# A two-layer graph network on one core: input rows turned by 32x32 blocks on the vector engine instead of by matmul, and head 0's value parts packed

## The reference

```
feats = einsum('bnf,hfu->bhnu', x, W0)
e_self, e_neigh = feats . a_self, feats . a_neigh              # per head and node
dense  = leaky_relu(e_self[i] + e_neigh[j], 0.2) + (-1e10) * (1 - adj[i, j])
x = layernorm(x + relu(softmax_j(dense) @ feats + bias))        # layer 0
agg = (adj @ x) / max(rowsum(adj), 1e-6)
x = layernorm(x + relu(concat([x, agg]) @ W1.T))                # layer 1
```

## Time and profile before

| | us |
|---|---|
| median of 3 runs | 3260.62 |
| profiled execution, its own time | 3259.45 |
| span of its profile | 3257.7 |
| PE busy | 3198.1 (98%) |
| PEld busy | 2698.7 (83%) |
| DVE busy | 2351.7 (72%) |
| ACT busy | 2095.9 (64%) |
| POOL busy | 283.6 (9%) |

### The profile page before, as it was taken

The page is one execution under the profiler, slowest core; times in us unless marked ns, Lnnn a source line. Parts: engine busy times, 40 slices in busy tenths (PEclk is TensorE's granted clock), DMA queues, the critical chain, the costliest instruction groups (busy, mean ns, idle before and its releaser), DMA issues.

```text
span 3257.7 us, 124901 instructions
## 1 busy us (share of the span) xinstructions
PE 3198.1 (98%) x56896; PEld 2698.7 (83%) x56896; DVE 2351.7 (72%) x4272; ACT 2095.9 (64%) x2712; POOL 283.6 (9%) x251
## 2 busy tenths in 40 slices
PE   7999999999999999999999999999999999999998
PEld 6969789697896978979788797987969879697895
DVE  6858678586785857859588585876858768586685
ACT  5748567485674947749477494765837658485583
POOL 0010200102011020100202002020020200202001
PEclk8999999999999999999999999999999999999999
DMA  6143151431524225251242513415144251331512
GB/s 217 58 114 102 51 159 66 109 98 51 154 68 118 87 60 157 62 133 65 78 141 63 140 56 94 129 58 146 51 102 120 58 147 62 102 115 51 140 33 49
DMA packets 368657, 314.52 MB, mean 97 GB/s; under 512 B 285056, under 2 KB 285056, under 8 KB 368128
## 3 DMA queue, kind: packets, MB, share of 16 engines
q1 hardware_dynamic: 368128, 306.52, 33.8%
HBM read 205.26 MB, written 34.08 MB: 73 GB/s over the span
## 4 chain that ended last, share of the span: by engine, by line
PE 89%; DVE 6%; issue 2%; ACT 2%; DMA 1%; SPq 0%; DVEq 0%; POOL 0%; ACTq 0%
PE six L940 77%; PE pair L940 11%; DVE mask L769 2%; PE six L964 1%; DVE rest L674 1%; PE pair L964 1%; DVE x_parts L669 1%; ACT step L512 1%; DMA s_bc<-self_scores 1%; ACT trh L477 0%; DVE x_parts L697 0%; DVE trl L708 0%; DMA self_scores<-sc_row 0%; DVE feat L699 0%; DVE trl L905 0%
## 5 line engine op out<-in xcount | busy, mean ns | idle before, releaser
L940 PE MATMUL six<-rows_bf,mask 128*128 128x65 bf16 x45056 | 1507.8, 193 | 19.3 <-DVE mask L769 12.6
L940 PEld LDWEIGHTS six<-rows_bf,mask 128*128 128x128 fp8e4 x45056 | 1497.6, 97 | 27.5 <-DVE mask L769 16.0
L512 ACT ACTIVATE step<-s_bc,n_step 128x1024 uint16<-128x1024 f32 x1024 | 1090.3, 1136 | 90.7 <-DVE mask L769 71.3
L769 DVE TENSOR_TENSOR mask<-adj_t,step 128x1024 uint16<-128x1024 uint16 x1024 | 655.2, 685 | 47.9 <-ACT step L512 47.4
L940 PE MATMUL six<-adj_t,x_parts 128*128 128x512 fp8e4 x1536 | 385.5, 380 | 11.1 <-DVE trl L905 5.4
L455 POOL TENSOR_TENSOR s_bc<-feat,rden 128x512 f32<-128x512 f32 x112 | 124.1, 1113 | 2721.3 <-DVE s_bc L818 2707.1
L940 PEld LDWEIGHTS six<-adj_t,x_parts 128*128 128x128 f16 x1536 | 145.9, 98 | 201.5 <-DVE trl L905 13.2
L477 ACT ACTIVATE mask<-six,rdeg 128x512 f32<-128x512 f32 x128 | 87.9, 686 | 237.5 <-PE six L940 237.5
L940 PE MATMUL six<-w1h,trh 128*128 128x512 f32 x512 | 211.6, 413 | 0.0
L477 ACT ACTIVATE trh<-six 128x512 fp32r<-128x512 f32 x160 | 87.9, 598 | 184.5 <-PE six L940 162.4
L940 PE MATMUL six<-w1h,trl 128*128 128x512 f32 x512 | 201.0, 392 | 0.0
(11 more groups left out here) (127 smaller groups left out, 4922.8 us busy)
## 6 DMA issues: line engine op xcount, KB each, us to landing
s_bc<-self_scores SPq DMA_DIRECT2D x128, 512.0 KB, 3.8
mask<-in_adj_dram SPq DMA_DIRECT2D x64, 512.0 KB, 4.1
adj_nat<-in_adj_dram SPq DMA_DIRECT2D x64, 512.0 KB, 3.5
xs<-in_x_dram SPq DMA_DIRECT2D x128, 256.0 KB, 3.9
out_dram<-mask SPq DMA_DIRECT2D x128, 256.0 KB, 3.3
adj_nat<-in_x_dram SPq DMA_DIRECT2D x64, 256.0 KB, 5.8
step<-in_x_dram SPq DMA_DIRECT2D x64, 256.0 KB, 4.2
xs<-in_L_gnn_W_dram SPq DMA_DIRECT2D x1, 2048.0 KB, 13.2
```

The lines of the kernel that those rows point to most:

```text
L512: act.activation(step[:, g % STEP_SLOTS], s_bc[:, h % 2], ACT.Sigmoid, scale=STEP, bias=n_step[:, jt, h:h + 1]).then_inc(stepped.sem, 1)
L769: dve.tensor_tensor(mask[:, g % MASK_SLOTS], adj_t[:, jt, :], step[:, g % STEP_SLOTS], ALU.logical_shift_left).then_inc(masked.sem, 1)
L940: return pe.matmul(o, l, r, start=start, stop=stop, skip_group_check=True)
```

## The change

Three things are changed, and what hangs on them.

1. A tile of x is loaded by 4 DMAs (one for each block of 128 features, on 32 partitions, as pieces of 128 values) in place of 1, so that after turning each 32x32 block in place the tile has features on its partitions, in a permuted order: partition 32k+s and chunk c hold feature 128k+32c+s. W0 is loaded in the same order by 16 DMAs in place of 4. DVE turns the tile in place (`turn_blocks`, one instruction); `turn_x` is gone from PE. `x_high` and `x_low` read SBUF in place of PSUM. `turn_blocks` stands after mask g for g in the new `TURN_AT` = (13, 21, 29, 37), `x_high` after step g+5, `x_low` after mask g+2; for tiles 4 to 7 it stands in layer 1's loop at t = 1, 2, 5 and 6.
2. `load_adj(b+1, s)` waits for `x_low` of the lead tiles, and stands after the loads of scores for heads 4 and 6 in place of 3 and 4. In the prologue DVE turns tiles 0 to 3 ahead of splitting W0.
3. ACT packs head 0's value parts too: the first halves of two parts ahead of step 0, the second halves ahead of step 8. PE waits for them at key tiles 0 and 4.

```diff
-    TURN_AT = (10, 13, 18, 21)
+    TURN_AT = (13, 21, 29, 37)
+    SPLIT_BEHIND = 2
+    TAIL_TURN_AT = (1, 2, 5, 6)
+    Q = P // KC
+        def turned_rows(t):
+            rows_of = lead_x[:, t] if t < HALF else tail_x[:, t - HALF]
+            return rows_of.rearrange("p (i c r) -> p c i r", i=KC, c=KC)
+        def by_blocks(rows_of):
+            return rows_of.rearrange("p c (i r) -> p c i r", i=KC)
...
+            def load_blocks(rows_of, b, t, landed):
+                for k in range(KC):
+                    sp.dma_start(rows_of[k * Q:(k + 1) * Q].rearrange("p (i f) -> p i f", i=KC),
+                                 x[b, t * P:(t + 1) * P, col(k)].rearrange("(i r) f -> r i f", i=KC)
+                                 ).then_inc(landed.sem, 16)
             for c in range(KC):
-                sp.dma_start(w_raw[:, c, :].rearrange("p (h u) -> p h u", h=H),
-                             gat_w[:, col(c), :].rearrange("h p u -> p h u")).then_inc(w_in[0], 16)
+                for k in range(KC):
+                    features_at = k * P + c * Q
+                    sp.dma_start(w_raw[k * Q:(k + 1) * Q, c, :].rearrange("p (h u) -> p h u", h=H),
+                                 gat_w[:, features_at:features_at + Q, :].rearrange("h p u -> p h u")
+                                 ).then_inc(w_in[0], 16)
...
-                    if h in (3, 4):
-                        s = h - 3
-                        sp.wait_ge(xt_ps.sem, xt_ps.at(b + 1, 2 * s + 2))
+                    if h in (4, 6):
+                        s = h // 2 - 2
+                        sp.wait_ge(xt_lo.sem, xt_lo.at(b + 1, 2 * s + 2))
                         load_adj(b + 1, s)
...
+                all_turned(act, b)
+                for part in range(PARTS - 1):
+                    pack_half(0, 0, part)
                 for g in range(H * T):
+                    if g == STEP_SLOTS + 4:
+                        for part in range(PARTS - 1):
+                            pack_half(0, 1, part)
...
                     make_step(g)
-                    if more and g - 9 in TURN_AT:
+                    turned_at = g - STEP_SLOTS - 1
+                    if more and turned_at in TURN_AT:
...
+            def turn_blocks(b, t):
+                source, landed = (lead_x[:, t], lead_in[t]) if t < HALF else (tail_x[:, t - HALF], tail_in[t - HALF])
+                dve.wait_ge(landed.sem, landed.at(b, 16 * KC))
+                dve.transpose(source, source).then_inc(x_turned_ok.sem, 1)
...
                     mask_word(g)
-                    if more and g - 7 in TURN_AT:
-                        x_low(b + 1, TURN_AT.index(g - 7))
+                    if more and g in TURN_AT:
+                        turn_blocks(b + 1, TURN_AT.index(g))
+                    if more and g - SPLIT_BEHIND in TURN_AT:
+                        x_low(b + 1, TURN_AT.index(g - SPLIT_BEHIND))
...
+                    if more and t in TAIL_TURN_AT:
+                        turn_blocks(b + 1, HALF + TAIL_TURN_AT.index(t))
...
             for t in range(HALF):
+                turn_blocks(0, t)
+            weight_parts()
+            for t in range(HALF):
                 x_low(0, t)
             attention_weights()
...
-                    if h >= PACKED_FROM:
-                        pe.wait_ge(val_packed.sem, val_packed.at(b, 2 * h + 2 if h > 1 else 2))
+                    pe.wait_ge(val_packed.sem, val_packed.at(b, 2 * h + 6 if h > 1 else 4 * h + 2))
...
-                        if more and h * T + jt in TURN_AT:
-                            turn_x(b + 1, TURN_AT.index(h * T + jt))
...
-                    if more and HALF <= t < T - 1:
-                        turn_x(b + 1, t)
-                    if more and t == T - 2:
-                        turn_x(b + 1, T - 1)
```

More of the change, by code:

```diff
@@ L216, in gat_sage_kernel @@
         x_in = [Signal(sem(f"x_in{t}"), 16) for t in range(T)]
-        lead_in = [Signal(sem(f"lead_in{t}"), 16) for t in range(HALF)]
-        tail_in = [Signal(sem(f"tail_in{t}"), 16) for t in range(HALF)]
+        lead_in = [Signal(sem(f"lead_in{t}"), 16 * KC) for t in range(HALF)]
+        tail_in = [Signal(sem(f"tail_in{t}"), 16 * KC) for t in range(HALF)]
         a_in = [Signal(sem(f"a_in{s}"), 32) for s in range(4)]
@@ L484, in x_high @@
             def x_high(b, t):
-                act.wait_ge(xt_ps.sem, xt_ps.at(b, t + 1))
-                copy(trh[:, :, col(t % HALF)],
-                     bank[XT_BANKS[t]][:].rearrange("p (k n) -> p k n", k=KC)).then_inc(xt_hi.sem, 1)
+                act.wait_ge(x_turned_ok.sem, x_turned_ok.at(b, t + 1))
+                copy(by_blocks(trh[:, :, col(t % HALF)]), turned_rows(t)).then_inc(xt_hi.sem, 1)
             def adj_words(b, t):
@@ L518, in pack_values, with pack_half @@
                         copy(packed[:, part, h % 2], val[h % 2][part]).then_inc(val_packed.sem, 1)
-                def pack_half(i, part):
+                def pack_half(h, i, part):
                     made = (val_f32, val_rest)[part]
                     tiles = (FIRST, SECOND)[i]
-                    act.wait_ge(made.sem, made.at(b, 3 + i))
-                    copy(packed[:, part, 1, :, tiles], val[1][part][:, :, tiles]).then_inc(val_packed.sem, 1)
+                    act.wait_ge(made.sem, made.at(b, 2 * h + i + 1))
+                    copy(packed[:, part, h, :, tiles], val[h][part][:, :, tiles]).then_inc(val_packed.sem, 1)
                 def weight_exp(o, a, k):
@@ L539, in batch @@
                     if behind in HALVES_AT and HALVES_AT[behind][1] < PARTS - 1:
-                        pack_half(*HALVES_AT[behind])
+                        pack_half(1, *HALVES_AT[behind])
                     make_step(g)
-                    if more and g - 9 in TURN_AT:
-                        if g - 9 == TURN_AT[0]:
+                    turned_at = g - STEP_SLOTS - 1
+                    if more and turned_at in TURN_AT:
+                        if turned_at == TURN_AT[0]:
                             act.wait_ge(ft_ps.sem, ft_ps.at(b, T))
-                        x_high(b + 1, TURN_AT.index(g - 9))
+                        x_high(b + 1, TURN_AT.index(turned_at))
                 def x1_parts_of(t):
@@ L632, in _, with weight_parts @@
         def _(dve):
[L634 to L637, removed]
+            def weight_parts():
+                dve.wait_ge(w_in[0], 16 * KC * KC)
+                dve.tensor_copy(w0h[:], w_raw).then_inc(w_ready, 1)
+                dve.wait_ge(w_ready, 1)
+                dve.tensor_tensor(w0l[:], w_raw, w0h[:].bitcast(F32), ALU.subtract).then_inc(w_ready, 1)
             def attention_weights():
@@ L928, in _ @@
                 feature_rows(0, t)
+            for t in range(HALF, T):
+                turn_blocks(0, t)
             for t in range(HALF, T):
@@ L956, in split_product @@
                 return ins
-            def turn_x(b, t):
-                source, landed = (lead_x[:, t], lead_in[t]) if t < HALF else (tail_x[:, t - HALF], tail_in[t - HALF])
-                pe.wait_ge(landed.sem, landed.at(b, 16))
-                if t % HALF >= 2:
-                    pe.wait_ge(xt_lo.sem, xt_lo.at(b, t - 1))
-                for k in range(KC):
-                    ins = pe.transpose(bank[XT_BANKS[t]][:, col(k)], source[:, col(k)], ident[:])
-                ins.then_inc(xt_ps.sem, 1)
             def features(b, t, chunks=range(KC)):
@@ L1012, in key_tile @@
                     sides = (high_bytes(words), low_bytes(words))
-                    parts = val[h % 2]
-                    if h >= PACKED_FROM:
-                        parts = [packed[:, part, h % 2] for part in range(PARTS)]
+                    parts = [packed[:, part, h % 2] for part in range(PARTS)]
                     for q in queries:
@@ L1129, in batch @@
                         own(t + 1)
-                    if more and HALF <= t < T - 1:
-                        turn_x(b + 1, t)
-                    if more and t == T - 2:
-                        turn_x(b + 1, T - 1)
             pe.wait_ge(consts, N_CONST)
-            for t in range(HALF):
-                turn_x(0, t)
             pe.wait_ge(w_ready, 2)
@@ L1143, in _ @@
             pe.wait_ge(ft_sb.sem, ft_sb.at(0, 2))
-            for t in range(HALF, T):
-                turn_x(0, t)
             pe.wait_ge(w_in[3], 16)
```

21 lines of the change are left out of this document (9 added, 12 removed).

## The result

The changed kernel takes 3272.8 us (median of 7 runs, 3270.7 to 3276.8); the kernel before took 3260.65 in 7 runs beside it. The ratio is 1.0043, 95% interval 1.0034 to 1.0053: slower by 0.4%, a small difference but clear of the noise. The profiled execution of after took 3275.75 us (span 3274.0), 16.3 above that of before (span 3257.7).

The account below looks back on a forecast made before the run. PE sets the time nearly everywhere, except in attention stretches where VectorE sets the pace. Profiled 3259.45 + 29 (attention) - 26 (tail) + 8 (prologue) + 0.3 (last batch) = 3270.7; the median lies 1.2 higher: 3272 us, range 3250 to 3300.

Parts of the forecast that it names:

- The cycle: Attention: VectorE takes 12.6 us per head over PE's 11.6, with 1.2 idle at x_low; 1.95 us a batch lost, +29.
- the queue keeps ahead: Attention: ACT's copy is ready when VectorE reaches x_low, cycle 11.4 us, 58 us go, 3211 us; chance 0.12.
- The turn: One in-place turn of a tile on VectorE takes 0.60 us start to start.
- cheap (0.3): A VectorE turn takes 0.3 us, cycle 12.3, 18 us go, 3254 us; chance 0.12.
- dear (1.15) turn: A VectorE turn takes 1.15 us, as two passes, 33 us more, 3305 us; chance 0.11.
- Tail tiles: Layer 1's loop: four turns leave PE, 1.75 us a batch counted in full, -26 us over 15 batches.
- The tail gives nothing: Layer 1's loop: the turn at t = 5 or 6 holds the addition and PE; 3298 us; chance 0.06.
- Packing: Head 0: PE waits 1.6 us at tile 4, almost wholly absorbed; first x_low 0.4 later; last batch loses 0.3.
- The start: Prologue: 32 issues at 0.5 us precede tile 3's last piece, features start at 24.4 us; +8, bounds +3 and +23.
- the longer start: Prologue: at 0.98 us an issue the start is 15 us later still, 3287 us; chance 0.11.
- The chances: Whole kernel: faster 0.19, same 0.19 (3254.1 to 3267.1 us), slower 0.62, shared out from the forecast's 0.48 and the rivals.

Follow-up runs that it names:

- run 1: The changed kernel with x_low of a lead tile behind mask g+4 instead of g+2: 3220.9 us, ratio 0.9878 to the kernel before.
- run 2: The changed kernel with x_low of a lead tile behind mask g+3 instead of g+2: 3240.7 us, ratio 0.9933 to the kernel before.
- run 4: The changed kernel without packing head 0, its value parts read in place: 3266.2 us, ratio 1.0019 to the kernel before.
- run 5: The kernel before with head 0's packing alone added: 3270.4 us, ratio 1.0029 to the kernel before.
- run 10: The changed kernel with x_low behind mask g+4, head 0's second halves packed ahead of step 6, and run 6's prologue: 3214.4 us, ratio 0.9857.
- run 6: The changed kernel with W0 split behind tile 0's turn and x's tail loads behind the first adjacency rows and W1: 3272.4 us, ratio 1.0038.
- run 9: The kernel before with its x_low two masks later and its third and fourth PE turns three tiles later: 3248.8 us, ratio 0.9958.
- run 8: The kernel before with lead tiles of batches 1 to 15 loaded by 4 DMAs a tile in 128 B runs: 3266.9 us, ratio 1.0010.

## Why the prediction was right

It said 3272 us and 62% slower; 3272.8 was measured. By its steps:

*The cycle,* 12.6 us with a wait of 1.2 at each `x_low`: measured 12.61, with 1.14, and 1.50 at the first. Tile 45 was to start 71.0 us after tile 0 (536.8 less 465.82), and did at 70.97. Runs 1 and 2 show the cause: shortening the wait by 0.61 us, and then taking it away, gives 2.37 and 3.93 us a batch against after. The rival "the queue keeps ahead" had tile 45 at 532.8, 4.0 us sooner than the forecast's 536.8, and 3.9 us a batch off the 200.82 of before, a period of 196.9; 197.31 came in run 1. That rival failed on its condition, since `x_low` did wait 1.14 us, and its price was sound.

*The turn,* 0.60 us: measured 0.63 start to start, 704 ns in the groups by shape:

```profile
L739 DVE STREAM_TRANSPOSE adj_nat<-adj_nat 128x512 f32<-128x512 f32 x64 | 45.1, 704 | 16.0 <-DMA adj_nat<-in_x_dram 16.0
```

The rivals of a cheap (0.3) and a dear (1.15) turn both fall. The Trainium skill ("Vector Engine (DVE) Microarchitecture Reference", The reshape front-end and per-opcode configuration) has this mode at one element per cycle and lane; the prediction's estimate of 0.71 us, made from it and from the figure for 128 columns, agrees with the 704 ns.

*Tail tiles,* -1.75 us a batch: measured -1.82, in full. "The tail gives nothing" falls.

*Packing,* 1.6 us at tile 4, nearly all absorbed, and 0.4 us on the first `x_low`: the stall (1.52) and the 0.36 us (1.50 less 1.14) came, but the absorption was over-stated. (The 0.4 does not follow from the terms it is given with: 1.06 less 0.43 is 0.63. The rest went where step g+5 would have waited for mask g+1 anyway.) Runs 4 and 5 have 0.65 and 0.61 us a batch left, 10 and 9 us in 15 batches, where the sum had 0.4 a batch in the attention and 0.3 in the last.

*The start,* +8: measured +9.8. SP took 0.49 and 0.47 us an issue (7.84 for 16, 5.67 for 12), as taken (0.5), and the longer start falls. Features began at 23.0 us and not 24.4; but from there to `w1_low` it took 22.4 us, not 19.3. The step that the sum left out is ACT's queue: its copies of the turned tail tiles began at 41.55, after it had stood 4.76 us for an adjacency transpose, and VectorE stood 2.04 us for the first of them. The two errors, 1.4 us and 3.1 us, partly cancel.

*What the sum did not have:* tile 0 starts 18.31 us after the last x36 run, where it was 18.10. PE's last product is now sooner there by the turns, but not the scores' way through memory, so that tile 0 waits 0.31 us for mask 0: 0.2 us a batch, 3 in all. And gaps of PE without a releaser: those at tile 4 aside, they grew from 7.4 to 11 us over the run (35.3 less 16 x 1.52). The sum from the profiled execution was +11.3; that execution shows +16.3, and the medians +12.2. So the steps missed 5 us of their own execution, 3 in the batches (+3 forecast, +6.2 measured) and 2 at the start. That the median lies within 1 us of the forecast is luck in part, by the 4 us between these two differences.

*The chances* do not add up quite: by the rules that the prediction states they are 0.18 for faster, 0.18 for same and 0.64 for slower, not 0.19, 0.19 and 0.62.

## What to carry to other kernels

A wait on a queue that is already the slowest costs its full length each time, as long as that queue stays the slowest: one constant (how many masks stand ahead of `x_low`) moved this change from 0.4% slower to 1.2% faster, and it could be read off the timeline, since the wait is printed there. Before pricing a wait away, look up the total of that releaser in the waits view (14.2 us here, for a promise of 36), and count into the other engine's cycle what else it does there. A stall that is taken away ahead of a stretch in which another engine leads comes back as a wait for that engine (runs 4 and 10). And loads moved along one queue take their issues with them: 16 small ones took 7.5 to 12 us here, in front of whatever came next.

## What the runs showed of the hardware

- In-place turning of 128x512 fp32 in 32x32 blocks takes VectorE 704 ns, about the time of a subtraction of that size (692).
- An issue of a 32-partition DMA took SP 0.47 to 0.49 us at the start. The 16 for x's tail tiles took 7.45 us there and 11.63 in run 6, where they stand further back in the same queue: the same instructions, 1.6 times as long. Inside a batch 16 such issues took 8.56 and 10.03. What makes them longer was not tested.
- TensorE stands still for 0.2 to 1 us at times with nothing named that it waits for; the total was 7.4 us (20 times) before, 13.0 (25) in run 9 and 13.6 (30) in run 8, in one profiled execution of each. Run 8 moves more DMA packets (487 thousand against 369), but in run 9 it grew with no more of them. What it is was not found.
